# The Perceiver steps of a PixArt layer pair: scores and products in half steps, fills spread over all steps, and the output step moved behind the sums

## What is computed

```python
lat = layer_norm(latents, ln2_w, ln2_b) * (1.0 + scale) + shift      # 1024 x 128
kv_in = concatenate((layer_norm(x, ln1_w, ln1_b), lat))              # 7428 x 128
q = einsum('bld,ed->ble', lat, Wq)                                   # 16 heads of 64
k, v = split(einsum('bld,ed->ble', kv_in, Wkv), 2)
logits = einsum('bhqd,bhkd->bhqk', q * attn_scale, k * attn_scale)
w = softmax(logits, axis=-1)
out = einsum('bhqk,bhkd->bhqd', w, v)
return einsum('ble,de->bld', out, Wo)
```

## Time and profile before

| | us |
|---|---|
| median of 3 runs | 3919.25 |
| lowest, highest | 3917.64, 3923.6 |
| the profiled execution | 3922.75 |
| its span in the profile | 3921.0 |
| TensorE, VectorE, ScalarE, GpSimd busy | 3392.1, 2565.2, 1510.6, 1648.4 |

### The profile page before, as it was taken

The page is one execution under the profiler, slowest core; times in us unless marked ns, Lnnn a source line. Parts: engine busy times, 40 slices in busy tenths (PEclk is TensorE's granted clock), DMA queues, the critical chain, the costliest instruction groups (busy, mean ns, idle before and its releaser), DMA issues. The chain is left out here.

```text
span 3921.0 us, 51606 instructions
## 1 busy us (share of the span) xinstructions
PE 3392.1 (87%) x18323; PEld 1897.8 (48%) x18323; DVE 2565.2 (65%) x4185; ACT 1510.6 (39%) x1843; POOL 1648.4 (42%) x1064
## 2 busy tenths in 40 slices
PE   3896969568335699999999999999999999999977
PEld 2554636333232255555555555555555555555535
DVE  6887868655217877777777777777767767773221
ACT  4332323134220044444444444444444444444432
POOL 1222222211220056545555555546545655555750
PEclk8897979656665599999999999999999999999998
DMA  1000000000130000000000000000000000000000
GB/s 56 0 0 0 0 0 0 0 11 1 43 97 6 0 1 1 3 2 1 1 3 2 1 3 1 1 3 2 1 3 2 1 3 2 1 1 1 1 23 6
DMA packets 20389, 27.86 MB, mean 7 GB/s; under 512 B 5065, under 2 KB 12369, under 8 KB 20049
## 3 DMA queue, kind: packets, MB, share of 16 engines
q1 hardware_dynamic: 18832, 21.83, 1.7%
q0 software_dynamic: 1344, 3.15, 0.3%
HBM read 21.30 MB, written 3.67 MB: 6 GB/s over the span
## 5 line engine op out<-in xcount | busy, mean ns | idle before, releaser
L2078 POOL TENSOR_TENSOR pair_total_pool<-pair_total_pool,pair_probs 128x1024 f32<-128x1024 f32 (+2 forms) x456 | 1334.5, 2926 | 970.4 <-DVE pair_total L2042 929.6
L1965 ACT ACTIVATE pair_probs<-banks 128x1024 f32<-128x1024 f32 (+1 forms) x944 | 959.7, 1025 | 1153.7 <-PE banks L1859 1114.9
L1995 DVE TENSOR_REDUCE pair_peaks<-banks 128x1 f32<-128x512 f32 (+1 forms) x1680 | 1055.4, 668 | 290.2 <-PE banks L1840 246.0
L1883 PE MATMUL banks<-pair_probs,pair_values 128*64 128x512 f32 (+1 forms) x3776 | 863.1, 598 | 0.0
L1840 PE MATMUL banks<-pair_k_high,pair_q_high 64*128 64x512 f32 (+1 forms) x1920 | 780.5, 456 | 84.9 <-DVE pair_peaks L1988 50.1
L2042 DVE TENSOR_TENSOR pair_total<-pair_total,pair_probs 128x512 f32<-128x512 f32 x464 | 445.0, 959 | 226.4 <-POOL pair_total_pool L2078 163.7
L1840 PEld LDWEIGHTS banks<-pair_k_high,pair_q_high 64*128 64x128 f32 x1920 | 345.5, 196 | 423.5 <-issue 330.6
L1859 PE MATMUL banks<-pair_q_shift,pair_one_rows 64*128 64x512 f32 (+1 forms) x1888 | 482.1, 437 | 7.6 <-ACT pair_probs L1965 7.4
L1859 PE MATMUL banks<-pair_q_high,pair_k_high 64*128 64x512 f32 (+1 forms) x1888 | 474.5, 396 | 0.0
L1883 PEld LDWEIGHTS banks<-pair_probs,pair_values 128*64 128x64 f32 (+1 forms) x3776 | 249.5, 136 | 454.3 <-issue 410.1
L1859 PE MATMUL banks<-pair_q_high,pair_k_low 64*128 64x512 f32 (+1 forms) x1888 | 463.2, 394 | 0.0
(11 more groups left out here) (306 smaller groups left out, 3290.2 us busy)
## 6 DMA issues: line engine op xcount, KB each, us to landing
expert_w<-in_fc SPq DMA_DIRECT2D x32, 256.0 KB
context_rows<-in_ctx SPq DMA_DIRECT2D x10, 320.0 KB, 6.0
dense_w<-in_We SPq DMA_DIRECT2D x2, 1024.0 KB
experts_in<-expert_zeros SPq DMA_DIRECT2D x1, 1024.0 KB, 3.9
expert_b<-in_fc_b SPq DMA_DIRECT2D x2, 512.0 KB, 4.7
expert_rows<-experts_in SPq DMA_DIRECT2D x16, 64.0 KB, 2.0
experts_out<-expert_result POOLq DMA_DIRECT2D x4, 256.0 KB, 3.8
row_parameters<-in_rows SPq DMA_DIRECT2D x1, 896.0 KB, 7.8
```

Of the source, the lines that this page charges most:

```text
L1883: last = pe.matmul(out[heads[head], c, :], values[0:n, (g * BLOCKS + i // 4) % 2, i % 4, heads[head]], probs_of(i)[0:n, c, head, :], start ...
L1965: act.activation(probs_of(i)[0:n, c], slot(e)[0:n], ACT.Exp, scale=1.0 / 8.0).then_inc(S["expd"].sem, 1)
L1995: v.reduce_max(peaks[:, head, t, b:b + 1], fill_banks(f)[:, head, 0:width(b)], axis=AX).then_inc(S["peaked"].sem, 1)
L2078: pool.tensor_tensor(pooled[0:rows_, first:3], pooled[0:rows_, first:3], probs_of(i)[0:rows_].rearrange("p c h n -> p (c h) n")[:, first + ...
```

## The change

The order list is rewritten, and nothing is computed otherwise. In the new list a step has two halves: two score units and the products of one tile, then two more units and the products of the other. `produce` stands before the second tile's products. Each of the four units of steps 0 to 28 carries one fill, and steps 16, 18, 20 and 22 have a fifth behind their units (116 + 4 = 120); before, steps 0 to 25 had four each, steps 26 and 27 eight. The fills' places inside a unit are new (`PLACES`: both halves first, or behind one and three passes). Keys are produced one block earlier from step 12 on, which takes one more slot of the key ring. `peak` and `shift` move from step 28 to step 29. Reciprocals come one in each of steps 1 to 8 rather than two in each of steps 1 to 4, and the output comes in step 10 behind the sums rather than in step 7 ahead of them.

```diff
--- before.py
+++ after.py
@@ -1587,15 +1587,24 @@
 BLOCKS = -(-KEYS // BLOCK)
 TILES = KEYS // P
 STEPS1 = TILES // 2
-RING1 = BLOCKS + 2
+RING1 = BLOCKS + 3
 assert TILES % 2 == 0 and STEPS1 == 2 * (BLOCKS - 1) + 1 and KEYS - TILES * P == REST
 
 
 CHUNKS = 8
-BOTH = ((("fill", 0), (1, 0), (0, 0), (1, 1), (0, 1), ("fill", 1), (0, 2), (1, 2), (0, 3), (1, 3)),
-        ((0, 0), (1, 0), ("fill", 0), (1, 1), (0, 1), (1, 2), (0, 2), ("fill", 1), (0, 3), (1, 3)),
-        ((0, 0), (1, 0), (0, 1), (1, 1), ("fill", 0), (1, 2), (0, 2), (1, 3), (0, 3), ("fill", 1)),
-        ((0, 0), (1, 0), (0, 1), (1, 1), (0, 2), (1, 2), ("fill", 0), (1, 3), (0, 3), ("fill", 1)))
+FIFTH = (16, 18, 20, 22)
+EXTRA = 12
+assert STEPS1 * 4 + len(FIFTH) == BLOCKS * TT
+PLACES = ((0, 0), (1, 3), (0, 0), (1, 3))
+
+
+def turns_of(place):
+
+    lanes = [[(head, m) for m in range(4)] for head in range(2)]
+    for head in range(2):
+        lanes[head].insert(place[head], ("fill", head))
+    return [turn for both in zip(*lanes) for turn in both]
+
 
 
 def perceiver_order():
@@ -1610,28 +1619,24 @@
     order += [("peak", 0), ("shift", 0)]
     for g in range(PAIRS):
         more, most = g + 1 < PAIRS, g + 2 < PAIRS
+        ahead = [("fill", g + 1, b, t) for b in range(BLOCKS) for t in range(TT)] if more else []
         for s in range(STEPS1 + 1):
             tiles = (2 * s, 2 * s + 1) if s < STEPS1 else (TILES,)
-            fills = []
-            if more and s < 2 * (BLOCKS - 2):
-                fills = [("fill", g + 1, s // 2, 4 * (s % 2) + n) for n in range(4)]
-            elif more and s < 2 * (BLOCKS - 1):
-                fills = [("fill", g + 1, BLOCKS - 2 + s % 2, t) for t in range(TT)]
             parts = [(i, c) for i in tiles for c in range(2)]
-            inside = len(fills) // 4
-            for n, (i, c) in enumerate(parts):
-                own = fills[n * inside:(n + 1) * inside] if inside else []
-                order.append(("scores", g, i, c, own[0] if own else None))
-                order += own[1:]
+            for i, c in parts:
+                order.append(("scores", g, i, c, ahead.pop(0) if ahead and s < STEPS1 else None))
+                if s and i % 2 == 0 and c == 1:
+                    order.append(("add", g, 2 * s - 2))
+            if ahead and s in FIFTH:
+                order.append(ahead.pop(0))
             if s % 2 == 1 and s < 2 * (BLOCKS - 2):
-                order.append(("produce", g + 1 if more else None, s // 2 + 1, g, s // 2 + 1))
-            elif s == 2 * (BLOCKS - 2) and more:
-                order.append(("produce", g + 1, BLOCKS - 1, None, None))
+                order.append(("produce", g + 1 if more else None, s // 2 + (1 if s < EXTRA else 2), g, s // 2 + 1))
+            elif s == EXTRA and more:
+                order.append(("produce", g + 1, s // 2 + 1, None, None))
             elif s == 2 * (BLOCKS - 2) + 1:
                 order.append(("produce", None, None, g, BLOCKS - 1))
-            elif s == STEPS1 - 1 and more:
+            elif s == STEPS1 and more:
                 order += [("peak", g + 1), ("shift", g + 1)]
-            elif s == STEPS1 and more:
                 if most:
                     order.append(("queries", g + 2))
                 order.append(("produce", g + 2 if most else None, 0, g + 1, 0))
@@ -1639,14 +1644,15 @@
                 if g:
                     order += [("denominators", g - 1), ("add", g - 1, TILES), ("evacuate", g - 1)]
             else:
-                order += [("add", g, 2 * s - 2), ("add", g, 2 * s - 1)]
-            if s == 7 and g:
+                order.append(("add", g, 2 * s - 1))
+            order += [("sum", g, i, c) for i, c in parts]
+            if 1 <= s <= CHUNKS and g:
+                order.append(("invert", g - 1, s - 1))
+            if s == CHUNKS and g:
+                order.append(("scale", g - 1))
+            if s == CHUNKS + 2 and g:
                 order.append(("output", g - 1))
-            order += [("sum", g, i, c) for i, c in parts]
-            if 1 <= s <= CHUNKS // 2 and g:
-                order += [("invert", g - 1, 2 * s - 2), ("invert", g - 1, 2 * s - 1)]
-            if s == CHUNKS // 2 and g:
-                order.append(("scale", g - 1))
+        assert not ahead
     g = PAIRS - 1
     order += [("denominators", g), ("add", g, TILES), ("evacuate", g)]
     order += [("invert", g, n) for n in range(CHUNKS)] + [("scale", g), ("output", g)]
@@ -1860,7 +1866,7 @@
 
                     turns = [(head, m) for m in range(4) for head in range(2)]
                     if f is not None:
-                        turns = BOTH[i % 2 * 2 + c]
+                        turns = turns_of(PLACES[i % 2 * 2 + c])
                     final = [turn for turn in turns if turn[0] != "fill"][-1]
                     for turn in turns:
                         if turn[0] == "fill":
```

## The result

The changed kernel takes 3992.22 us (median of 4 runs, 3989.37 to 3994.86) against 3919.66 (4 runs, 3917.64 to 3923.6): ratio 1.0184, interval 1.0166 to 1.0201, 72.6 us slower. The forecast was 3989, in a range of 3945 to 4018. Differences in us are taken from these two medians; each experiment's ratio comes from executions of the kernel before made beside it (their medians are 3918.7 to 3922.05). One execution of e1 was slow (4470.48 us at a granted clock of 0.71, all others 0.90 to 0.91): its median is 3877.0 with it and 3876.67 without, and the ratio leaves it out.

The account below looks back on a forecast made before the run. TensorE sets the pace, with VectorE's reductions pacing steps 26 and 27. Groups 1 to 6 at +11.7 us each (70), group 0 +8, group 7 -5, less 3 for shorter reductions, give +70: 3989 us, range 3945 to 4018.

Parts of the forecast that it names:

- The late sums: VectorE's sums, covered by only 1.84 us of products, delay the next step's first reduction; even steps behind odd ones lose 0.81.
- The clean half: Undisturbed half step on TensorE, two score units with fills and one tile's products: 4.37 us.
- gain 0.16 a step: Steps in halves, if nothing else moves: even 8.74 us against 8.90, odd 10.69 against 10.84.
- plain pair: An even and an odd step with fills: 20.34 us against 19.74, +0.6.
- Reciprocals: Steps 1 to 8: each of eight costs its full 0.84 us behind the sums; net +5.1 a group.
- Fifth fills: Steps 16, 18, 20, 22: each waits for four reductions, +1.17 us and 0.1 in the step behind; +5.1 a group.
- Key block: Extra key block in step 12: about half a produce, 1.0 us, and 0.7 more in step 13; +1.8.
- The output: Moved behind the sums: before it cost 3.76 us, now 2.1 and 0.5 of delay; -1.2 a group.
- Steps 26 to 0: End of a group: steps 26 and 27 -7.4 us, step 28 +0.8, step 29 -0.3, step 0 +0.6; sum -6.3.
- Rival 1: Late sums are absorbed: pairs gain 0.32 us, about -7 a group, 3869 us in all; chance 0.07.
- rival 3: VectorE falls behind for good: delays pile up from step to step, a pair costs over 1 us; 4030 us; chance 0.05.
- rival 2: Stalls partly made good: loss per pair 0.2 us rather than 0.6, reciprocals cost half; 3945 us; chance 0.10.

Follow-up runs that it names:

- e1: Changed kernel with halves undone (both tiles' products behind the four units) and the fills' old places restored; 3877.0 us, ratio 0.988 to the kernel before.
- e2: Changed kernel with a step's sums moved behind the next step's first two units, ahead of that half's products; 3928.2 us, ratio 1.0015 to before.
- e5: e2 with the group's maxima ahead of the late sums in step 29 and GpSimd's scale behind those of step 9; 3883.63 us, ratio 0.9905 to before.
- e10: e1 with the new places of the fills; 3957.25 us, ratio 1.0102 to before.
- e7: Kernel before with only the output moved, to step 10 behind the sums; 3900.16 us, ratio 0.9952 to before.
- e3: Changed kernel with each reciprocal done on one of its 128 columns only; 3950.18 us, ratio 1.0071 to before.
- e4: Changed kernel without the four fifth fills a group and their reductions; 3958.15 us, ratio 1.0095 to before.
- e6: e1 with the fifth fills moved behind the first tile's products and the sums, ahead of the second tile's products; 3854.68 us, ratio 0.9828 to before.

## Why the prediction was right, and where its sum was off

- **The late sums.** D, the time from a step's start to its first reduction, was forecast at 1.43 and 0.68; the rows have 1.41 and 0.65 (2810.73 less 2810.08). The step's first products were to start after 3.34 us and did after 3.41. Moving the sums and what they collided with (e2, e5) took 108.6 us away; giving the cover back, with the old places (e1), took 115.2, and with the new ones (e10) 35.0, because these cost 80 of their own without halves. This cause is shown from both sides.
- **The clean half** was sized at 4.37 and is 4.41 (2805.67 to 2810.08). Two of them are 8.82, which would gain 0.08 a step and not 0.16; and beside fills even that does not come: e5 has steps of 8.92 and 10.87 against 8.90 and 10.85. Only group 7, without fills, keeps a gain, 3.3 us in 28 steps or 0.12 each. So the "gain 0.16 a step" is the term that was sized wrong, and with it a plain pair costs 0.79 (20.54 against 19.75), not 0.6.
- **Reciprocals**: 0.84 each forecast, 0.79 and 0.81 measured (10.45 and 11.69 against 9.66 and 10.88).
- **Fifth fills**: 1.17 and 0.1 forecast, 1.18 and 0.19 measured. **Key block**: 1.8 forecast; steps 12 and 13 took 10.74 and 11.64, 1.84 more than their neighbours.
- **The output was mis-sized.** I held the interval of 14.60 against an odd step's 10.84, but between the products of steps 7 and 8 lies an even one, 8.90. Before, the output cost 5.7; after, steps 10 and 11 take 23.13, 2.6 over a plain pair. It gained 3.1 a group, not 1.2; e7, by itself, shows 3.3.
- **Steps 26 to 0** gained 7.9, not 6.3. Steps 26 and 27 fell by 8.0 (7.4 forecast). Step 28 fell from 9.15 to 8.07 where I had it grow by 0.8, since what it lost with the shift was more than four fills of 260 columns. Step 29, which took over the shift, grew from 9.78 to 10.50 where I had it shrink by 0.3.
- Together a group lost 10.3 instead of 11.7. Group 0 lost 7.9 (8 forecast), the 28 steps of group 7 gained 3.3, not 5. From the stage's first exponential to its last step that is 67.5 us; the remaining 4.6 us of the two profiled spans' 72.1 lie mainly in the last stage, whose code is the same. The windows of it, before and after:

```profile
3787.00:3921.00 134.00, 91.94 (x456) 61.97 (x452) 31.39 (x99) 28.70 (x27) 10.43 (x5) 0.79 0.07 21
```

```profile
3855.90:3993.00 137.10, 93.64 (x448) 62.26 (x444) 31.40 (x99) 28.37 (x27) 11.05 (x6) 0.77 0.06 21
```

  The granted clock differs by 0.02 there. In e3 and e4, which keep the changed order, the same stretch takes 131.1 and 137.2 us, at 0.79 and 0.77, so I do not put these us down to the change.
- So the forecast's closeness, 3 us, owes something to luck: errors of opposite sign (pairs dearer by 2.3 a group, output and end cheaper by 3.5), and some 4 us of the last stage that the sum did not have.
- **Rivals.** Rival 1 (absorbed) is refuted by the late reductions; rival 3 (falling behind for good) by VectorE's 1.77 us idle in each step; rival 2 (0.2 a pair) by the 0.79 a pair. It had a true core for the kernel before only, where the exponential's wait swallowed part of a stall.
- By the Trainium skill, "TensorE: Matmul & The Clock Gate", LDWEIGHTS, the two more turns of a step between scores and products were 0.21 us as an estimate, against 0.3 from the rows. The trace does not bear the lower price out: with halves of 4.41 instead of 4.37 even the rows' price was 0.08 a step too low.

## What to carry to other kernels

An engine's slack counts where its queue lets it be used. VectorE was 27% idle in a group, but its sums stood behind the fills of a step's second half, so cutting the cover behind them from 3.58 to 1.87 us stalled TensorE once a step while VectorE idled 1.8 us later in that step. When work on the pacing engine is split, list for each helper what must end between its last input and the next request for its buffer, and compare that with the cover that is left.

Spreading the fills and reciprocals, moving the output, and the halves came in one change. The first two together were worth 43 us (e1; the output alone 19.5 in e7), 65 with the fifth fills put better (e6), and the halves cost more. Take such a bundle apart before you judge it, and not by adding up: halves cost 35 or 169 us depending on where the fills stood. Nor is the last word on halves spoken: e5 still had its fifth fills at 1.1 us each, and no run combines its late sums with the fifth fills of e6.

When you hold an interval against a neighbour, check that both are of the same kind: even and odd steps differ by 2 us here.

## What the runs showed of the hardware

Some operations of VectorE do not run beside one of GpSimd. In e2 two sums that take 2.01 us took 3.44 while GpSimd's `scale` ran (2389.89 to 2392.25), and so in six groups; 1.43 us are what was left of that operation when the sums started, within 0.15.

The second operation of `peak`, on 16 columns, shows it more sharply, in both kernels. Ahead of group 0, with GpSimd idle, it takes 0.17 us; at the end of each later group it starts 0.2 behind a GpSimd addition and ends with it, within 0.04. In e5 it met the longer addition and took 3.50 in five groups, 0.17 in the two in which it did not start behind it. Whether this delays a step is not shown. VectorE's timeline of the changed kernel, both cases:

```profile
1368.18 0.17 DVE L2032 TENSOR_SCALAR pair_peak_columns<-pair_peak_columns 128x16 f32<-128x16 f32 x1
2635.66 2.20 DVE L2032 TENSOR_SCALAR pair_peak_columns<-pair_peak_columns 128x16 f32<-128x16 f32 x1
```

GpSimd's timeline beside the second:

```profile
2635.45 2.38 POOL L2084 TENSOR_TENSOR pair_total_pool<-pair_total_pool,pair_probs 128x1024 f32<-128x1024 f32 x1 [3.03 <-DVE pair_total L2048]
```

Others are not held up: in the changed kernel reductions from PSUM ran beside GpSimd's additions in their usual 0.63 to 0.69, and reciprocals in 0.94 to 0.95. The Trainium skill, "SBUF — State Buffer", Terms, says that VectorE and GpSimd share a port pair that is locked for a whole instruction, so that the loser is fully blocked. For the sums beside `scale`, the trace agrees.
